# First mixer of a two-layer kernel: tiles traded between batches, another form of softplus, gates and output sums moved

## The reference

```python
z = x @ W_z.T
params = x @ W_params.T                       # 64 columns for dt, 16 for B (unused), 16 for C
dt = softplus(params[..., :64] @ W_dt.T + b_dt)
u = silu(causal depthwise conv of x with conv_w, 4 taps)
A = -exp(A_log)                               # 256 channels x 16 states
A_tilde = exp(dt[..., None] * A)
B_tilde = where(abs(A) < 1e-5, dt[..., None], (A_tilde - 1) / (A + 1e-10))
h[0] = B_tilde[0] * u[0]
h[t+1] = A_tilde[t] * h[t] + B_tilde[t] * u[t]
y = einsum(C, h) + u * D
out = (y * silu(z)) @ W_out.T
```

## Time and profile before

| what | us |
|---|---|
| median of 3 runs (3598.51 to 3606.71) | 3601.9 |
| profiled execution, its own time | 3600.97 |
| its span | 3599.2 |
| PE busy in the span | 2852.6 (79%) |
| VectorE busy | 2831.8 (79%) |
| GpSimd busy | 2280.4 (63%) |
| ScalarE busy | 1817.9 (51%) |

### The profile page before, as it was taken

One profiled execution on the slowest core, in us unless ns is written; L12 is line 12 of the kernel. 1 busy time (PEld: TensorE's weight loads), 2 busy tenths in 40 slices (PEclk: granted clock), 3 DMA queues, 4 the chain that ended last, 5 costly groups with the idle time before them and its releaser, 6 DMA issues. The chain is left out here.

```text
span 3599.2 us, 26475 instructions
## 1 busy us (share of the span) xinstructions
PE 2852.6 (79%) x7878; PEld 1208.1 (34%) x7878; DVE 2831.8 (79%) x2234; ACT 1817.9 (51%) x2447; POOL 2280.4 (63%) x1094
## 2 busy tenths in 40 slices
PE   5677766765657888898888788798897887689899
PEld 2222222354212333333333333233333332244344
DVE  4899799643349999999999999999999999455300
ACT  4566477322354555555655656555655554333311
POOL 3598299200219889889899899898889898100000
PEclk8799789888869989989899999999999999899999
DMA  1011011155524444545454455444544555301000
GB/s 58 16 53 47 8 47 47 46 187 211 187 69 170 161 173 164 171 174 169 163 180 165 173 177 175 166 175 169 182 174 166 182 181 198 113 30 36 12 18 24
DMA packets 164651, 451.40 MB, mean 125 GB/s; under 512 B 23328, under 2 KB 52192, under 8 KB 164480
## 3 DMA queue, kind: packets, MB, share of 16 engines
q1 hardware_dynamic: 158752, 428.79, 34.6%
q0 software_dynamic: 5760, 20.97, 1.5%
HBM read 414.85 MB, written 34.87 MB: 125 GB/s over the span
## 5 line engine op out<-in xcount | busy, mean ns | idle before, releaser
L1379 POOL TENSOR_TENSOR mix_prod<-mix_spread,mix_h 128x1024 f32<-128x1024 f32 x512 | 1376.1, 2690 | 240.9 <-DVE mix_h L1785 125.7
L1879 PE MATMUL mix_banks<-mix_prod,kept_ident 128*128 128x512 f32 x2048 | 1053.4, 641 | 77.7 <-POOL mix_prod L1379 55.0
L1429 ACT ACTIVATE mix_side_in<-mix_dt,mix_neg_a 128x1024 f32<-128x1024 f32 x384 | 437.6, 1141 | 313.3 <-DVE mix_h L1785 310.0
L1879 PEld LDWEIGHTS mix_banks<-mix_prod,kept_ident 128*128 128x128 f32 x2048 | 406.0, 203 | 515.4 <-issue 304.5
L1771 DVE TENSOR_TENSOR mix_banks<-mix_banks,mix_dtu 128x1024 f32<-128x1024 f32 x384 | 467.5, 1217 | 10.8 <-PE mix_banks L1869 6.2
L1785 DVE TENSOR_TENSOR_SCAN mix_h<-mix_side_in,mix_state,mix_banks 128x1024 f32<-128x1024 f32 x192 | 450.7, 2347 | 18.5 <-issue 0.9
L1785 DVE TENSOR_TENSOR_SCAN mix_h<-mix_side_in,mix_banks 128x1024 f32<-128x1024 f32 x192 | 439.0, 2287 | 19.5 <-ACT mix_side_in L1429 1.8
L1869 PE MATMUL mix_banks<-mix_parts,kept_sel 96*128 96x512 bf16 x768 | 249.0, 408 | 255.3 <-DVE mix_h L1785 247.1
L1389 POOL TENSOR_TENSOR mix_side_in<-mix_spread,mix_dtu 128x512 f32<-128x512 f32 x256 | 337.2, 1317 | 0.1
L435 POOL TENSOR_TENSOR mix_drive<-mix_drive,mix_du 128x1024 f32<-128x1024 f32 x128 | 305.2, 2400 | 41.2 <-ACT mix_drive L500 40.8
L638 DVE TENSOR_TENSOR_SCAN mix_h<-mix_banks,mix_state,mix_drive 128x1024 f32<-128x1024 f32 x128 | 296.2, 2339 | 24.3 <-POOL mix_drive L435 22.1
(11 more groups left out here) (259 smaller groups left out, 4406.2 us busy)
## 6 DMA issues: line engine op xcount, KB each, us to landing
mix_spread<-c_rows SPq DMA_DIRECT2D x640, 512.0 KB, 3.8
mix_c_row<-c_rows SPq DMA_DIRECT2D x40, 512.0 KB, 3.6
exa_f<-f SPq DMA_DIRECT2D x32, 512.0 KB, 6.6
slot_outputs<-exa_inter POOLq DMA_DIRECT2D x32, 512.0 KB, 7.2
ln_zp<-slot_outputs SPq DMA_DIRECT2D x8, 2048.0 KB, 10.5
first_acc<-xT SPq DMA_DIRECT2D x8, 512.0 KB, 3.6
x_scratch<-first_acc POOLq DMA_DIRECT2D x8, 512.0 KB, 3.5
fw_scratch<-mix_res SPq DMA_DIRECT2D x8, 512.0 KB, 6.2
```

Source lines behind the costliest of these rows:

```text
L1379: pool.tensor_tensor(prod[:, un % 2, :], spread[:, i % SLOTS, :], h[:, un % HR, :], ALU.mult).then_inc(prod_ready, 1)
L1429: act.activation(drive[un % 2] if pooled(un) else side_in[:, un % 2, :], dt[:, at // NS, :], ACT.Exp, scale=neg_a[:, way(p), at:at + 1]).t ...
L1879: mm = pe.matmul(y_bank[:, hf, :], k.ident[:], half(prod[:, un % 2, :], hf), start=False, stop=True, skip_group_check=True)
```

## The change

- The hardware loop over b becomes a Python loop, so both batches are written out, in all five queues.
- `u` and `dt` become two tiles `turns`: batch 0 has u in the first and dt in the second, batch 1 the other way round. So ACT's first tap of batch 1 waits for the last scan alone; the waits for all sums and the output projection move in front of softplus.
- Softplus: ACT computes 1 + exp as one more pass (into dt's place), DVE makes (1 + exp) - 1 - exp, subtracts it from the logarithm and adds the maximum; GpSimd has no part in it. `lg` lies in `h` alone, `off` is gone.
- The gates of z move from before the run into it, in front of ACT's second decay. `masked(0)` starts when half of `shape` and all of softplus are done.
- PE's order: dt of groups 0, 1 (which need `dtin` only), row sums 0, 1, dt of 2, 3, z of 0, 1, row sums 2, 3 after the first half of `shape`, z of 2, 3 after the whole.
- The four output sums of batch 0 stand between and behind the taps of batch 1; those of batch 1 stay at the end.

```diff
-        u = m.sb("u", [P, C, L + 1])
-        dt = m.sb("dt", [P, C, L + 1])
+        turns = [m.sb(f"turn{j}", [P, C, L + 1]) for j in range(B)]
...
+        def u_of(b):
+            return turns[b % 2]
+        def dt_of(b):
+            return turns[1 - b % 2]
...
 (pool)
-            with pool.Fori(0, B) as b:
-                def log_add(g):
-                    pool.wait_ge(log_done, b * G + (g + 1))
-                    pool.wait_ge(soft_step, b * 2 * G + 2 * (g + 1))
-                    pool.tensor_tensor(lg[g % 2], lg[g % 2], off[g % 2], ALU.add).then_inc(log_sum, 1)
-
+            for b in range(B):
+                u = u_of(b)
                 for c in range(C):
-                    log_add(H2 * c)
-                    log_add(H2 * c + 1)
                     pool.wait_ge(u_first, b * C + (c + 1))
                     pool.tensor_tensor(du[:, c, :], u[:, c, 1:L + 1], u[:, c, 0:L], ALU.subtract).then_inc(du_ready, 1)
...
 (act)
                 act.wait_ge(r.scan_done, CREDIT + b * UNITS)
-                act.wait_ge(r.sum_done, CREDIT + b * UNITS)
-                act.wait_ge(out_ready, 1 + b * G)
...
                 act.preload_act_table_set("natural_log_exp_and_others")
+                act.wait_ge(r.sum_done, CREDIT + b * UNITS)
+                act.wait_ge(out_ready, 1 + b * G)
...
                     act.activation(ex[s], ex[s], ACT.Exp, scale=-1.0).then_inc(exp_done, 1)
+                    act.activation(part(dt, g, 1), ex[s], ACT.Identity, bias=one[:, 0:1]).then_inc(one_more, 1)
                     act.activation(lg[s], ex[s], ACT.Ln, bias=one[:, 0:1]).then_inc(log_done, 1)
-                act.preload_act_table_set("silu_and_others")
-                for g in range(G):
-                    act.wait_ge(z_ready, b * G + (g + 1))
-                    if g == 2:
-                        act.wait_ge(soft_done, b * G + G)
-                    act.activation(part(zs, g), flatb[...z_bank[g]...], ACT.Silu).then_inc(gate_ready, 1)
-                act.preload_act_table_set("natural_log_exp_and_others")
-                act.wait_ge(step_ready, b + 1)
+                def gates():
+                    act.preload_act_table_set("silu_and_others")
+                    for g in range(G):
+                        act.wait_ge(z_ready, b * G + (g + 1))
+                        if g == 0 and b:
+                            act.wait_ge(gated, b * G)
+                        act.activation(part(zs, g), flatb[...z_bank[g]...], ACT.Silu).then_inc(gate_ready, 1)
+                    act.preload_act_table_set("natural_log_exp_and_others")
...
+                act.wait_ge(soft_done, b * G + G)
+                act.wait_ge(step_ready, b * C + 1)
                 masked(0)
                 for i in range(UNITS):
+                    if i == 0:
+                        act.wait_ge(step_ready, b * C + C)
+                    if i == 1:
+                        gates()
...
 (dve)
                         dve.scalar_tensor_tensor(out=uc, in0=k.xn[:, c, b, t:t + L], ...).then_inc(tap_done, 1)
+                    if b:
+                        add_out(b - 1, 2 * c)
+                        add_out(b - 1, 2 * c + 1)
...
                 def step_size(g):
+                    s, n = g % 2, b * G + g
+                    now = part(dt, g, 1)
+                    dve.wait_ge(one_more, n + 1)
+                    dve.scalar_tensor_tensor(out=now, in0=now, scalar=-1.0, in1=ex[s], op0=ALU.add,
+                                             op1=ALU.subtract).then_inc(soft_step, 1)
+                    dve.wait_ge(log_done, n + 1)
+                    dve.wait_ge(soft_step, 2 * n + 1)
+                    dve.tensor_tensor(lg[s], lg[s], now, ALU.subtract).then_inc(soft_step, 1)
+                    dve.wait_ge(soft_step, 2 * n + 2)
+                    dve.scalar_tensor_tensor(out=now, in0=lin[s], scalar=0.0, in1=lg[s], op0=ALU.max,
+                                             op1=ALU.add).then_inc(soft_done, 1)
...
 (pe)
+                if b:
+                    pe.wait_ge(added, 3 + b * G - 2)
                 (the parameters' matmuls)
-                pe.wait_ge(par_kept, b * 2 + 2)
-                pe.wait_ge(added, 3 + b * G)
+                if b:
+                    pe.wait_ge(added, 3 + b * G)
+                pe.wait_ge(par_kept, b * 2 + 1)
...
+                step_rows(0)
+                step_rows(1)
+                pe.wait_ge(par_kept, b * 2 + 2)
+                row_sums(0)
+                row_sums(1)
+                step_rows(2)
+                step_rows(3)
+                gate_rows(0)
+                gate_rows(1)
+                pe.wait_ge(step_ready, b * C + 1)
+                row_sums(2)
+                row_sums(3)
+                pe.wait_ge(step_ready, b * C + C)
+                gate_rows(2)
+                gate_rows(3)
                 pe.wait_ge(sel_built, 4)
                 pe.wait_ge(split, b * 5 + 5)
                 pe.wait_ge(gate_ready, b * G + G)
```

More of the change, by code:

```diff
@@ L367, in mixer0 @@
         rs_bank = [0, 2]
[L369 to L370 removed]
+        lin, ex, lg = ([r.drive[:, 0, :], r.prod[:, 0, :]], [r.drive[:, 1, :], r.prod[:, 1, :]],
+                       [r.h[:, 0, :], r.h[:, 1, :]])
         mid, rest = dd[0:32, 0, 0:L // 2].bitcast(BF16), dd[0:32, 1, :]
         (loaded, cleared, ea_ready, setup, rs_turned, rs_kept, tap0, tap_done, u_ready, par_ready, par_kept, split,
[L374 removed]
+         dt_ready, abs_done, exp_done, one_more, log_done, soft_step, soft_done, u_first, du_ready, shaped, step_ready,
          rs_ready, mask_ready, saved, z_ready, gate_ready, y_step, gated, out_ready, added, sel_built,
@@ L458, in _ @@
                            ACT.Copy).then_inc(rs_kept, 1)
-            with act.Fori(0, B) as b:
+            for b in range(B):
+                u, dt = u_of(b), dt_of(b)
                 act.wait_ge(r.scan_done, CREDIT + b * UNITS)
-                act.wait_ge(r.sum_done, CREDIT + b * UNITS)
-                act.wait_ge(out_ready, 1 + b * G)
                 for c in range(C):
@@ L557, in _, with add_out @@
             dve.wait_ge(setup, SETUP)
-            with dve.Fori(0, B) as b:
+            def add_out(b, n):
+                hf, c = n // C, n % C
+                dve.wait_ge(out_ready, 1 + b * G + (n + 1))
+                ac = acc[:, c, b * L + hf * TC:b * L + (hf + 1) * TC]
+                dve.tensor_tensor(ac, flat(banks[:, 2 * n:2 * n + 2, :]), ac, ALU.add).then_inc(added, 1)
+            for b in range(B):
+                u, dt = u_of(b), dt_of(b)
                 for c in range(C):
@@ L574, in _ @@
                     dve.tensor_copy(u[:, c, 0:1], u[:, c, 1:2]).then_inc(u_first, 1)
+                if b:
+                    dve.wait_ge(saved, b * C * NS)
                 for c in range(C):
@@ L592, in step_size @@
-                def step_size(g):
-                    dve.wait_ge(log_sum, b * G + (g + 1))
-                    dve.scalar_tensor_tensor(out=part(dt, g, 1), in0=lin[g % 2], scalar=0.0, in1=lg[g % 2], op0=ALU.max,
+                def step_size(g):
+                    s, n = g % 2, b * G + g
+                    now = part(dt, g, 1)
[7 more added lines that the diff above has]
+                    dve.scalar_tensor_tensor(out=now, in0=lin[s], scalar=0.0, in1=lg[s], op0=ALU.max,
@@ L666, in _ @@
                 gate_y(G - 1)
-                for n in range(G):
-                    hf, c = n // C, n % C
-                    dve.wait_ge(out_ready, 1 + b * G + (n + 1))
-                    ac = acc[:, c, ds(b * L + hf * TC, TC)]
-                    dve.tensor_tensor(ac, flat(banks[:, 2 * n:2 * n + 2, :]), ac, ALU.add).then_inc(added, 1)
+            for n in range(G):
+                add_out(B - 1, n)
         @block.tensor
@@ L682, in _ @@
             pe.wait_ge(rs_kept, 1)
-            with pe.Fori(0, B) as b:
-                pe.wait_ge(added, 3 + b * G - 2)
+            for b in range(B):
+                u, dt = u_of(b), dt_of(b)
+                if b:
+                    pe.wait_ge(added, 3 + b * G - 2)
                 for q in range(4):
@@ L689, in _, with step_rows @@
                 mm.then_inc(par_ready, 1)
-                pe.wait_ge(par_kept, b * 2 + 2)
-                pe.wait_ge(added, 3 + b * G)
-                for g in range(G):
+                if b:
+                    pe.wait_ge(added, 3 + b * G)
+                pe.wait_ge(par_kept, b * 2 + 1)
+                def step_rows(g):
                     c, hf = blocks[g]
@@ L707, in row_sums, with gate_rows @@
                     mm.then_inc(rs_ready, 1)
-                row_sums(0)
-                row_sums(1)
-                pe.wait_ge(soft_step, b * 2 * G + 2 * H2 + 1)
-                row_sums(2)
-                row_sums(3)
-                for g in range(G):
+                def gate_rows(g):
                     c, hf = blocks[g]
```

39 lines of the change are left out of this document (13 added, 26 removed).

## The result

The changed kernel takes 3588.17 us (median of 13 runs, 3581.36 to 3603.12) and the kernel before, run beside it, 3599.34 (13 runs, 3593.02 to 3608.51): a ratio of 0.9969, 95% interval 0.9958 to 0.9980. The forecast was 3598, the range 3587 to 3607. Repeated later beside other kernels it was 0.9977 [0.9963, 0.9991], and a copy of the kernel before, not changed at all, came out at 0.9982 [0.9965, 0.9998]. So about 0.2% is what two programs of one time can differ by here, and the change is worth 0.2 to 0.3%, at the edge of that. (A ratio is not the quotient of the two medians printed beside it: for the copy, 3597.12 over 3599.17 would be 0.9994.)

A forecast was written before the change was run, and what follows sets the result against it. VectorE and GpSimd were taken to bound the first mixer's scan runs, chains of waits its preludes. Terms +2.1 - 5.6 + 0.6 = -2.9 us from the profiled 3601.0 gave 3598.1; forecast 3598, range 3587 to 3607.

The forecast's parts named there:

- second rival: First mixer: TensorE recovers sooner (z at 2.4 GHz) or the run tightens through short hops; -11 us, 3590; chance 0.16.
- the sum of the preludes: Waits before each scan run, added up: second scan at 153.3 (+2.1 us) in batch 0, 448.9 (-5.6) in batch 1.
- T1: End of VectorE's last step before the first scan run; forecast at 135.9 us, against 139.81 before.
- The rival that it holds nothing up: Preludes: GpSimd's first drive doesn't delay VectorE's second shape product; 2.3 us saved twice, -7.5, 3593; chance 0.20.
- S - T: From VectorE's last step before a scan run to the run's second scan; forecast 17.4 us, 5.5 to 6 more than before.
- The rival with both at the low level: Gates inside the run: z of groups 2 and 3 both at low clock, 13.8 us; +9 in all, 3607; chance 0.10.
- The drain of the tables: ScalarE's table loads inside the run: about 1.38 us of draining per switch, 5.5 more for both batches; left out.
- the second sum, +2.6: The forecast's total for the change if draining at ScalarE's table switches added 5.5 us; the sum used was -2.9.
- the rival in which the loads hold ScalarE longer: Gates' four table loads on the path each take 1.28 us more; +5.1, giving +2.2, 3603; chance 0.03.
- Between the runs: From batch 0's last product to batch 1's second scan: split starts 7.1 us earlier; second scan 448.9 against 454.51, -5.6.
- the change leaves what they do per unit alone: Scan runs of the first mixer: VectorE's and GpSimd's work per unit stays as before.
- +0.6 after S: After a run's second scan: later mask pass makes GpSimd's drive 0.3 us late at the sixth scan, for both batches.

The follow-up runs named there:

- e2: The kernel before with only its hardware loops over the batches in the first mixer written out; 3595.81 us, ratio 0.9992.
- e4: The changed kernel again, unaltered, for a second trace and ratio; 3591.24 us, ratio 0.9977 to the kernel before.
- e6: The changed kernel with the first mask pass, and so GpSimd's first drive, waiting for the whole of shape; 3594.99 us, ratio 0.9981 to the kernel before.
- e5: The changed kernel with TensorE computing z of group 1 four more times to fill its pause before z of group 2; 3593.05 us, 0.9983.
- e7: The changed kernel with batch 0's four output sums back at the end of the batch, ahead of batch 1's taps; 3601.28 us, 0.9997.
- e10: The kernel before with two extra matmuls on TensorE at each change of group, filling its pause there; 3598.09 us, ratio 0.9993.
- e11: e1 with extra TensorE matmuls both ahead of z and at the changes of group; 3565.93 us, ratio 0.9896 to the kernel before.
- e8: The kernel before again, unchanged, for a second trace; 3597.12 us, ratio 0.9982.
- e1: The changed kernel with z's gates back ahead of the run, z of groups 2 and 3 not waiting for shape's second half; 3569.47 us, 0.9913.
- e12: e1 again, unaltered, beside its variants; 3565.62 us, ratio 0.9906 to the kernel before.
- e3: The kernel before with the new softplus alone, its loops, tiles, gates and output sums kept; 3601.08 us, ratio 0.9997.
- e9: e1 with four extra TensorE matmuls between dt of groups 2 and 3; 3568.53 us, ratio 0.9905 to the kernel before.

## Why the prediction was right

- **The number.** That 3588.17 lies in the range of 3587 to 3607 is in part luck. The forecast was 2.9 us less, the medians differ by 11.2, and the measured time is near the fast end. It was given 0.59 that the difference stays under 7.2 us and 0.31 that the kernel gets faster by more; the second came. The second rival's 3590 is nearest, but not by its reasons: TensorE didn't recover sooner (z took 9.52 and 8.81), and writing out the loops, for which the forecast had bounds (0 to 3, 0 to 2) that no row showed, gives 1.8 (e2). What held is the sum of the preludes, term by term.
- **Softplus and the port.** T1 135.9 was forecast, 135.83 and (e4) 136.48 came. The two differences were charged 7.1 us of VectorE's time; in the first prelude 3.3 and 3.2 of it show, at L599 (3.72, before 0.38 for two) and L612 (4.43, where its twins take 1.23).
- **The drive inside shape.** Charged 2.3, measured 2.02 (4.31 less 2.29). The rival that it holds nothing up is dead, in both batches. e6, which removes the collision and gets the product back to 2.29, shows that the drive was the cause.
- **Gates inside the run.** S - T 17.4 was forecast, 17.76 and 17.03 came, in e4 17.55 and 18.10; z of groups 2 and 3 was put at 9.33 and took 9.52 and 8.81. e5 confirms the clock's share. The rival with both at the low level would have been 13.8 for z and over 18.9 for S - T. The drain of the tables isn't there: 138.06 to 139.37 holds the load alone, so the second sum, +2.6, was the wrong one, and the rival in which the loads hold ScalarE longer is dead with it.
- **Between the runs.** 92.7 (448.9 less the last product at 356.2) was forecast and 92.63 came; e4 has 93.71. e7 shows that the sums between the taps carry 3.9 to 5.0 of it. e2 shows that writing out the loop is worth 1.8; as forecast, it lay in the part that the taps beside the out projection replace, and doesn't come on top: splitting starts at ScalarE's copy, 27.75 us after the last product (forecast 383.95 - 356.19 = 27.76).
- **The step that failed** is "the change leaves what they do per unit alone", with its +0.6 after S. Run 1 became 3.3 us shorter in the first pair of traces and 2.1 in the second; run 2 0.4 shorter and 0.9 longer. The prediction had named a move of over 2 us in a run's length as a sign of being wrong, and here it is. The +0.6 didn't come either: the wait of 0.20 us in front of the sixth scan is there before, 12.85 us after S, and in after, 12.96 us after it. The waits for drives further on in run 1, 2.3 us before, are gone in after.

In run 1 of after, the slow stretch of TensorE comes right at the change of group, at all three of them, and is over before it can hold up ScalarE:

```profile
261.12 3.48 PE L769 MATMUL mix_banks<-mix_prod,kept_ident 128*128 128x512 f32 x4 [1.79 <-DVE mix_turn L673]
264.55 0.74 PE L763 MATMUL mix_banks<-mix_parts,kept_sel 96*128 96x512 bf16 x2
265.13 1.88 PE L769 MATMUL mix_banks<-mix_prod,kept_ident 128*128 128x512 f32 x4
```

Before, it was the second four that took 3.62. That the low clock behind the pause costs run 1 its 3.4 us is shown by e10, and by e11 in another kernel. The traces without that fill say more. I counted in each of their 24 runs at how many of the three changes of group the second four sums took 2.3 us or more, and not 1.88:

```
changes of group with slow second sums   runs   their lengths
none                                        3   201.5 to 201.8   (after, run 1; e6, both)
one                                         9   202.4 to 203.0
two                                        12   203.0 to 205.0
```

Before and e8 have two in run 1 and one in run 2; after has none and one, e4 one and two, e1 and e12 two and two. So the length of a run hangs on where the low stretch falls, in the kernel before and in the changed one alike, and it moves with small shifts ahead of the run: e6, which differs from after in what the first mask pass waits for and in nothing else, has none in both. What sets the place stays open. The loop (e2) and softplus (e3) alone leave run 1 at 204.45 and 204.57. Run 2, and the second traces of both kernels, say that it isn't a steady gain of the change.

By the mean of the two pairs: S1 +3.1 (forecast +2.1), run 1 -2.7 (0.3 forecast), "between" -5.1 (-5.6), run 2 +0.3 (+0.3), the tail -0.1 (0), together -4.6. Of the +3.1, 0.7 came in with the start of the prelude and isn't the change's: VectorE's first copy lies at 97.37 and 96.64 in the two traces of before, at 97.36 and 97.99 in those of after. The other 6.6 of the measured 11.2 us stand in no segment that the change touches, and no run here shows where they come from; they are about as much as the 0.18% (6.5 us) by which the unchanged copy came out sooner.

## What to carry to other kernels

A stretch that moves to another place on an engine's queue is to be priced by what stands behind it there: the gates cost 14 us in the first batch inside the run, and little ahead of it, where ScalarE idled while VectorE worked. The pieces of this change need each other as well (softplus alone raises S), and one piece was hiding the others' gain, so each is worth undoing by itself. Where an unchanged copy differs by 0.18%, compare lengths of segments in the traces and not medians, and take two traces of each kernel: the gain of 3.3 us in the first pair's run 1 was 2.1 in the second.

## What the runs showed of the hardware

TensorE's clock stayed low through long, unbroken work. In after, dt's matmuls (64 rows) and the row sums (16 rows) run back to back from 83.76 to 105.03, at a granted clock of 0.50 to 0.52, the 1.2 GHz level. z's matmuls, with 128 rows, begin at 110.46 and are at 1.00 (2.4 GHz) from 115 on. Three stretches, with columns as in the earlier trace rows:

```profile
97.80:105.00 7.20, 7.20 (x9) 2.50 (x8) 7.10 (x3) 4.80 (x5) 7.20 (x2) 0.50 0.01 2
...
115.00:119.60 4.60, 4.60 (x11) 1.70 (x9) 4.60 (x4) 3.96 (x4) 0.00 (x0) 1.00 0.00 0
...
384.80:389.00 4.20, 4.20 (x9) 1.38 (x8) 4.12 (x4) 4.18 (x3) 0.00 (x0) 0.85 0.40 125
```

TensorE is busy for the whole of each. The first and the third are 64 and 16 rows deep; the third follows work at full clock and loses some of it while busy. e9 met the same: behind its fill z was at 1.00, the 16-row sums after it were at 0.89 on average (403.0 to 407.1), and the next z started at 0.50. Few rows don't always mean the low level: the 64-row matmuls at 381.18 in after ran at 1.00. No run changes the number of rows alone, so that it is the cause is not shown.

And the engine that waited for the port of VectorE and GpSimd got it as soon as the other's running instruction ended, even between two back-to-back instructions: the drive issued at 127.85 in after ended at 131.30, 2.2 us after VectorE's first product, and the second product took 4.31.
